# VectorE's weighted down product moved to the head of its expert step

## The reference, cut to what matters

```python
xb = x[token_buf].reshape(E, CAP, H)                 # gather 192 token rows
gu = jnp.einsum('ech,ehf->ecf', xb, W_gate_up)       # up product: gate half g, other half u
g, u = jnp.split(gu, 2, axis=-1)
inter = jax.nn.silu(g) * u
yb = jnp.einsum('eci,eih->ech', inter, W_down)       # down product
yb = yb * w_buf.reshape(E, CAP, 1)                   # weighted by the routing weight
routed = jnp.zeros((T, H), x.dtype).at[token_buf].add(yb.reshape(E * CAP, H))   # scatter-add
```

## Time and profile before

| | us |
|---|---|
| median of 3 runs | 5136.79 |
| lowest and highest of them | 5110.01, 10328.97 |
| the profiled execution | 5124.69 |
| its span in the trace | 5122.9 |
| PE busy in the span | 4059.1 (79%) |
| DVE busy | 3587.1 (70%) |
| POOL busy | 3004.7 (59%) |
| ACT busy | 2093.4 (41%) |

### The profile page before, as it was taken

The page is one execution under the profiler, slowest core; times in us unless marked ns, Lnnn a source line. Parts: engine busy times, 40 slices in busy tenths (PEclk is TensorE's granted clock), DMA queues, the critical chain, the costliest instruction groups (busy, mean ns, idle before and its releaser), DMA issues. The chain is left out here.

```text
span 5122.9 us, 70166 instructions
## 1 busy us (share of the span) xinstructions
PE 4059.1 (79%) x19938; PEld 2853.9 (56%) x19938; DVE 3587.1 (70%) x6132; ACT 2093.4 (41%) x4195; POOL 3004.7 (59%) x1609
## 2 busy tenths in 40 slices
PE   3467877878787778887888788787776899989997
PEld 3334555545555455555455454555444788878886
DVE  2877787778777777878777877777852666656664
ACT  2555444445544444445445544544430222222221
POOL 1876666667665666656666666666630455555554
PEclk8568787778877787878777877778788999999999
DMA  3332222222232222223222222222210777777775
GB/s 85 74 80 64 66 77 69 76 67 75 65 85 65 64 65 66 76 65 84 65 64 75 67 76 70 65 64 58 73 31 26 186 186 184 183 178 183 185 184 125
DMA packets 243529, 473.38 MB, mean 92 GB/s; under 512 B 39644, under 2 KB 162080, under 8 KB 243220
## 3 DMA queue, kind: packets, MB, share of 16 engines
q1 hardware_dynamic: 203792, 429.90, 31.6%
q0 software_dynamic: 36864, 37.98, 4.5%
q10 hardware_dynamic: 2564, 1.82, 0.2%
HBM read 404.99 MB, written 64.56 MB: 92 GB/s over the span
## 5 line engine op out<-in xcount | busy, mean ns | idle before, releaser
L504 POOL TENSOR_TENSOR y<-y,state 128x972 f32<-128x972 f32 x448 | 1003.9, 2241 | 962.5 <-DVE state L633 956.4
L627 DVE TENSOR_TENSOR_SCAN ps<-ps,state 128x972 f32<-128x972 f32 x512 | 1112.1, 2182 | 123.2 <-ACT ps L527 61.1
L483 POOL TENSOR_TENSOR state<-du,b_rows 128x972 f32<-128x972 f32 x512 | 1181.7, 2325 | 7.5 <-POOL delta L494 7.1
L527 ACT ACTIVATE ps<-delta,a_neg 128x324 f32<-128x324 f32 x1536 | 734.8, 523 | 915.2 <-DVE state L633 896.1
L782 PE MATMUL ps<-ws_d,inter 116*98 116x192 f32 (+1 forms) x3072 | 600.7, 361 | 87.9 <-DVE h L638 54.1
L764 PE MATMUL ps<-x2f,ws_u 128*116 128x324 f32 x1024 | 447.9, 572 | 247.7 <-DVE ag L748 247.6
L782 PEld LDWEIGHTS ps<-ws_d,inter 116*98 116x98 f32 (+1 forms) x3072 | 559.5, 195 | 142.4 <-DVE h L638 64.6
L1025 POOL DMA_INDIRECT out_rows<-yo,scatter_idx x256 | 369.8, 1444 | 435.8 <-DMA out_rows<-yo,scatter_idx 361.5
L633 DVE TENSOR_TENSOR state<-ps,c_rows 128x972 f32<-128x972 f32 x512 | 589.2, 1161 | 7.5
L764 PE MATMUL ps<-x2f,ws_g 128*116 128x324 f32 x1024 | 452.6, 577 | 103.6 <-DVE inter L754 101.5
L754 DVE TENSOR_TENSOR inter<-ag,ps 116x648 f32<-116x648 f32 x256 | 211.2, 825 | 417.6 <-PE ps L767 416.8
(11 more groups left out here) (165 smaller groups left out, 6638.1 us busy)
## 6 DMA issues: line engine op xcount, KB each, us to landing
b_rows<-bc_rows SPq DMA_DIRECT2D x256, 324.0 KB, 6.1
c_rows<-bc_rows SPq DMA_DIRECT2D x256, 324.0 KB, 5.1
w_lo<-in_we_up SPq DMA_DIRECT2D x128, 348.0 KB, 4.0
w_down<-in_we_down SPq DMA_DIRECT2D x128, 348.0 KB
x_in<-in_x SPq DMA_DIRECT2D x32, 1176.0 KB, 8.2
w_hi<-in_we_up SPq DMA_DIRECT2D x256, 116.0 KB, 5.9
image_cnt<-running_counts SPq DMA_DIRECT2D x256, 81.0 KB
w_lo<-in_we_up SPq DMA_DIRECT2D x128, 116.0 KB, 4.3
```

Source lines behind the costliest of these rows:

```text
L483: nc.gpsimd.tensor_tensor(b.state[n % 4][:], b.du[t.p][:], row, ALU.mult).then_inc(input_ready, 1)
L504: nc.gpsimd.tensor_tensor(y, y, b.state[n % 4][:], ALU.add).then_inc(y_added, 1)
L527: ins = nc.scalar.activation(to[:, c * L:c * L + L], b.delta[t.p][:, c, :], ACT.Exp, scale=b.a_neg[:, c, k:k + 1])
L627: nc.vector.tensor_tensor_scan(s, s, b.state[k % 4][:].rearrange("p a t -> p (a t)"), 0.0, ALU.mult, ALU.add).then_inc(scan_done, 1)
```

## The change

In VectorE's list of the expert stage the piece `("down", 2)` goes from the fourth place to the first. The lag, the waits, the instructions and the other engines' lists are the same, so VectorE's step now is: `down` of i - 2, the two gate products of i, `weigh` of i, `token`, `one_hot`, `dot`.

```diff
 EXPERT_ORDER = {
     "sp": (("load_find", -7), ("load_up", -3), ("load_down", -3)),
     "pool": (("scatter", 2), ("token", -4)),
     "act": (("dot", 0), ("up", 0, 0), ("up", 0, 1), ("turn", -1)),
-    "dve": (("up", 0, 0), ("up", 0, 1), ("weigh", 0), ("down", 2), ("token", -5), ("one_hot", -6), ("dot", -1)),
+    "dve": (("down", 2), ("up", 0, 0), ("up", 0, 1), ("weigh", 0), ("token", -5), ("one_hot", -6), ("dot", -1)),
     "pe": (("up", 0), ("count", -5), ("turn", -1), ("down", 1)),
 }
```

## The result

The changed kernel takes 5158.14 us (median of 10 runs, 5141.76 to 5815.51) beside 5123.38 for the kernel before (10 runs): a ratio of 1.0069 [1.0046, 1.0093]. The 5815.51 ran at a lower clock throughout (0.61 on average against 0.82) and is left out of the ratio. By the bound of 2% this is no change, though the interval leaves out 1: the kernel is 0.7% slower.

What follows compares the result with a forecast made beforehand. PE was taken as the bound, with the scatter chain nearly level and binding after the move: 112 links x (9.10 - 8.76) = +38, less 9, gives +29 on 5124.69, so 5154 us; range 5040 to 5265.

Steps and rivals of the forecast that it cites:

- PE is the bound, with 0.78 us a step to win: Expert stage: PE's `down` waits 0.78 us for `yo`; without that, PE's step falls from 8.72 to 7.94 us.
- The scatter chain takes over: POOL's scatters each wait for the landing before, 8.76 us a link; PE at 7.94 would end up following this chain.
- 1.2: Idle time of PE's `down`, released by `yo`, expected in each step: about 9.1 - 7.9 = 1.2 us.
- rival B: Scatters land within 7.94 us and PE stays the bound: all 127 steps save 0.78, 5026 us; chance 0.16.
- `yo` starts when a scatter lands, and the loads go out 2.9 us after a scatter: At every step one landing drives VectorE, PE and POOL, with `w_down` 2.85 us after the scatter starts.
- The link of 9.10: Time from scatter to scatter in the new alignment, 9.10 us instead of 8.76: +38 us over 112 links.
- -9: Outside the 112 links, 12 of 15 links at start and end gain PE's 0.78 us: -9 us.
- No fall of the clock up to a link of 9.75: PE's clock stays up after waits to 1.81 us, so rows show no fall up to 7.94 + 1.81 = 9.75.
- C: VectorE's head-of-queue wait costs more than the gap: links of 9.55 to 11.15, 5204 to 5383 us; chance 0.32.
- constant fixed cost: Skill's rule for GpSimd-issued transfers: about 2.0 us plus bytes over 436 GB/s; it would give rival B's full gain.

Runs made afterwards that it cites:

- w_down_16_engines_new: New order with the w_down load issued as two transfers of 112 and 4 partitions; 4994.16 us, 0.9747 of the kernel before.
- half-padded kernel: New order with two idle matmuls ahead of PE's transposes in every step; 5141.39 us, 1.0038 of the kernel before.
- padded: New order with four idle matmuls, about 0.96 us, ahead of PE's transposes in every step; 5106.48 us, 0.9961 of the kernel before.

## Why the prediction was right, step by step

**1. PE is the bound, with 0.78 us a step to win: right, but too small.** Without the chain as rival, PE's step is 7.72, not 7.94 (w_down_16_engines_new). The idle column counts from the end of the last transpose; without the wait `down` begins before that end, which the column does not show.

**2. The scatter chain takes over: right.** The landing wait has 96 entries, and POOL's waits for landings stay (66, 229.3 us). PE's `down` is idle 0.82 us a step (86.4 over 106), not 1.2: the link is 0.11 shorter, and a `down` is busy for 3.09 us on average instead of 2.83 (328.0 over 106, 308.6 over 109), as some ran slowly. Taking the chain away gave 0.9807, as the sum for rival B had it.

**3. `yo` starts when a scatter lands, and the loads go out 2.9 us after a scatter: right for half of the links.** 2.94 and 2.86 us are in the rows (4206.85 - 4203.91, 4197.20 - 4194.34). 51 of the 112 links have 2.7 to 3.3, mean 9.58 us; the prediction had it at every step. Of the 41 links of 9.75 or more 23 are such; 14 follow the short link behind a slow `down`, with the next `w_down` 5.6 to 7.7 us behind the scatter; 4 begin at POOL's stops (last section).

**4. The link of 9.10: the mis-sized term.** It is 8.99, so 112 x (8.988 - 8.761) = +25.5 us instead of +38. The 9.10 was the mean of one link of 11.15 and six of 8.76 on average ((4583.51 - 4530.97) / 6), which is the mean before: how many links were taken in set the figure, so that it came so near is partly luck. Outside the stretch the span is 8 us shorter (17.4 - 25.5) where -9 was taken; 2.1 of that was there before the expert stage began. Together +17.4, forecast +29. That the median of 5158.14 lies so near the forecast owes something to chance as well: in the medians the difference is 35 us, in the profiled executions 17.

**5. No fall of the clock up to a link of 9.75: wrong.** The row at 4585.66 has one after 1.69 us of idle time, at the end of a link of 9.61 (4585.77 - 4576.16), and 21 of the 128 `down` took over 3.2 us. It seems not to have moved the sum, as the short link behind it gives back what the stop took: the three links around each of 18 of them have a mean of 8.86, the other 58 one of 9.11.

**Rivals.** B, scatters landing in time, did not come about here; with the load spread it does, at 4994 us. C had the right mechanism in its single links (41 of 9.75 or more) but not in the mean, since after each stop comes a short link. The landing shown above took 8.61 us; without loads one took 3.23 (chain of the kernel before, at 5102.72). That speaks again against the constant fixed cost that the Trainium skill gives (page "DMA: Bandwidth & Descriptors", section "Anatomy of one DMA — SWDGE (gpsimd) path").

**Open:** how the surplus of 8.99 over 8.68 is shared between the place of the loads and the slow `down`. Moving the loads won 0.19 and splitting them in halves 0.22, and both also brought fewer slow `down` (12 and 7, against 21). But with 10 slow `down` the half-padded kernel still has 8.96, so their number does not set the link. The start of `w_lo` behind the scatter (medians) goes with it better: 7.36 before, 7.15 padded and 6.98 moved have links of 8.68 to 8.80; 5.22 after and 5.27 half padded have 8.99 and 8.96. The two halves, 5.37 and 8.77, do not fit, so the cause is not shown.

## What to carry to other kernels

Before removing a wait, work out the pace of the next chain: here 8.76 us a link against PE's 8.72, so the gain could not arrive. Relieve that chain in the same edit, by looking at what shares its DMA engines: the reorder was worth 2.5% once one load no longer ran on a quarter of the DMA engines, and neither edit was worth anything alone. An engine that runs into such a chain can be slower than one that is paced a little under it (5158.14 against 5106.48 us).

## What the runs showed of the hardware

- A `down` of 4.49 us (4585.66) ran at a granted clock of 0.62 on average, so in part at the lower level (0.50, 1.2 GHz), after 1.69 us without work, though one ran at 2.4 GHz after 1.72 (4203.87) and another after 1.81. So the idle time just before does not decide alone.
- A partition count of 116 left `w_down` on a quarter of the engines; with two transfers of 112 and 4 partitions the DMA share of the stage was 0.86 instead of 0.76, and the traffic 208 GB/s instead of 178: the same bytes in less time.
- POOL stops for some 3 to 6 us ahead of a scatter, put down to "issue", every 29 steps (scatters 30, 59, 88 and 117): 255 us apart before, 260 after, and 224 where a step takes 7.72. It follows the work, not the time. The long wait of the earlier trace rows begins at such a stop; its cause stays open.
